# Residual loaded by the stages that use it, the last attention's weights loaded one stage earlier, and the output bias added inside the tile loop

## The chip, the cores and the metric

The kernel runs on 1 core of one Trainium2 chip. Its time is the device time of one execution in microseconds (us); several executions are taken and their median is compared.
## The reference, cut to what matters

The residual `x` is [2, 1024, 256] in float32, the context `ctx` [2, 77, 256]. Eight blocks follow, each added to the residual:

```
x = x + attn0(ln(x), ctx)          # 16 heads of 16, boolean mask: (softmax(q k^T / 4 + mask) v) Wo + bo
x = x + fp8_linear(ln(x))
x = x + attn1(ln(x), ctx)          # 16 heads of 64, keys and queries normalised
x = x + top2_experts(ln(x))        # 8 experts, the best 2 of each token
x = x + transformer(ln(x), ctx)    # self attention, cross attention, feed-forward, each with layer norm
x = x + choice_experts(ln(x))      # 8 experts, each takes its 1024 best tokens
x = x + attn3(ln(x), ctx)          # as attn0, float mask times -1e15
x = x + int8_feed_forward(ln(x))
```

The feed-forward at the end is written out to HBM as the result.

## The kernel before

**Stages.** The 2048 rows are 16 tiles of 128 (`NT`), a tile's row in `k.x` is 256 wide, and a group (`G`) is 4 tiles. `program` runs its stages one after the other, each a block of its own with one instruction stream per engine, written by hand; an engine runs its stream in order and waits on semaphores. Between two stages all engines meet: SP's stream must be over too, and then the stage's semaphores are cleared on POOL and all engines meet again (`Semaphores.clear`, L724 and L725). The whole residual stays in SBUF as `k.x`.

**The residual.** `load_residual` is a stage of its own: one DMA of 2 MB for `k.x` (L3407), seven constants (L3410), and a wait for all of them. The two stages with experts add their results by indirect DMAs into a table in HBM (`t2_total`, `ch_total`); when the last addition has landed, SP loads 2 MB back into `k.x` (L1149, L2414) and waits, and only then is the stage over. The next stages are `transformer_block` and the second `narrow_attention`. The transformer block starts on DVE with the layer norm's moments of four tiles (`first_moments`, L1976), and reads the other tiles four at a time later.

**The narrow attention** (`narrow_attention`, tags `L0_` and `L3_`) has a prologue and a tile loop. SP issues the weights first. In the prologue PE's stream is: keys and values (L3127, wait for `kv_loaded`); `turn_rows(0)` (L3118, transposes of the first group's normalised rows `h`); then for each group g: `queries(g)` (L3138), `turn_rows(g + 1)`, and `value_blocks` (L3155 and L3157), which needs `vbd` from POOL. DVE's stream is `normalise` of tiles 0 to 7 (statistics L3018 and L3021, then a chain of 12 small instructions in which each waits for the one before, L3025 and L742 to L751, then `h` at L3332), the masked keys `kbd` (L3339), and `normalise` of tiles 8 to 15. POOL clears `vbd` (L3303), copies `head_of` (L3304), builds `vbd` in four instructions (L3311) when the values are there, then adds the output bias `bo` to `x` in four instructions of a group each (L3319), each behind that group's `h`, and then enters the tile loop with one subtraction of the row maximum per tile (L3322). In the loop DVE takes the scores and finds the maxima three tiles ahead (L3357, L3365), divides and adds the result into `x` (L3380, which also waits for `bo_added`), and in the first attention it prepares the wide attention's weights beside it (`centre`, L95 to L107). In the first attention POOL's first `vbd` instruction has a change of its library in front (MODIFY_POOL_CONFIG, at 15.3 us).

Of the kernel before, what the change touches and what calls it, by code (L numbers as in the profile page):

```python
# [12 lines left out]
U8 = mybir.dt.uint8  # L13
# [661 lines left out]
class Attention:  # L675

    def __init__(self, tag, wq, wk, wv, wo, bo, bq, bk, bv, mask, mask_is_bool, beside=None):
# [3 lines left out]
        self.scale = 16 ** -0.5  # L682
# [399 lines left out]
def top2_experts(nc, k, i):  # L1082
    with ExitStack() as ctx:
# [5 lines left out]
        total = nc.dram_tensor("t2_total", (ROWS, D), F32, kind="Internal").ap()  # L1089

# [32 lines left out]
        restored = sem("restored")  # L1123
# [9 lines left out]
        def _(sp):  # L1133
# [15 lines left out]
            sp.dma_start(k.x[:], total[0:T, :].rearrange("(t p) d -> p t d", p=P)).then_inc(restored, 16)  # L1149
            sp.wait_ge(restored, 16)  # L1150
# [421 lines left out]
def transformer_block(nc, k, i):  # L1572
    scale = float(D) ** -0.5
    with ExitStack() as ctx:
# [32 lines left out]
        dve_chain, pool_chain = sem("dve_chain"), sem("pool_chain")  # L1607
        block = ctx.enter_context(nc.Block())
# [45 lines left out]
        def _(sp):  # L1654
            sp.dma_start(after[:], i["after128"]).then_inc(after_loaded, 16)
# [312 lines left out]
        def _(dve):  # L1968
# [21 lines left out]
            def first_moments(n):  # L1990
                rows = [k.x[:, unit(a)[0] * BT + unit(a)[1] + u, :] for a in (2 * n - 2, 2 * n - 1) for u in range(DUO)]
                if n >= 3:
# [353 lines left out]
def choice_experts(nc, k, i):  # L2346
    with ExitStack() as ctx:
# [5 lines left out]
        total = nc.dram_tensor("ch_total", (T, D), F32, kind="Internal").ap()  # L2353
        ps = ctx.enter_context(nc.psum_tensor("ch_ps", [P, 8, BANK], F32))
# [45 lines left out]
        restored = sem("restored")  # L2400
# [630 lines left out]
def narrow_attention(nc, k, a):  # L3031
# [3 lines left out]
    with ExitStack() as ctx:  # L3035
# [6 lines left out]
        wq, wk, wv = sb("wq_sb", [P, KC, D]), sb("wk", [P, KC, D]), sb("wv", [P, KC, D])  # L3042
        wo, bo, bq = sb("wo", [P, HC16, D]), sb("bo_sb", [P, D]), sb("bq_sb", [P, HC16])
        cols = sb("cols", [P, 2, HC16])
# [11 lines left out]
        n_masks = B if a.mask_is_bool else NT  # L3056
        neg = sb("neg", [P, n_masks, KEYS])
        if a.mask_is_bool:
            mask_u8 = sb("mask_u8", [P, B, KEYS], U8)
# [449 lines left out]
```

## Time and profile before

| | |
|---|---|
| median of 3 runs | 1848.33 us (1845.6 to 1849.25) |
| the profiled execution: its own time | 1844.21 us |
| its span in the trace | 1842.4 us |
| mean granted clock of TensorE | 0.87 |
| PE busy | 1444.0 us (78% of the span) |
| DVE busy | 1128.4 us (61%) |
| ACT busy | 747.4 us (41%) |
| POOL busy | 649.3 us (35%) |
| last attention, first DVE instruction to next stage's first | 1570.65 to 1730.01 us |
| transformer block, likewise | 870.40 to 1157.61 us |

The busy times are sums over stages with different limits; a change at a stage's edge is read from the timeline at that edge. The profiled execution took 1.8 us more than its span, and 4.1 us less than the median.

### The profile page before, as it was taken

To read this page: it belongs to the slowest core of one execution; us is meant where nothing else is said; L and a number is where in the kernel's file an instruction comes from. 1 tells how busy PE (TensorE), PEld (TensorE's weight loads), DVE (VectorE), ACT (ScalarE), POOL (GpSimd) and SP (SyncE) were. 2 spreads that over 40 slices of the span, in tenths; PEclk is the share of its full clock that TensorE was granted. 3 is DMA by queue.
4 is the path that set the end of the run, shared out by engine and by line. 5 is a ranking of instruction groups with operands and counts; after the bars stand their busy time and mean duration, and the time that the engine had idled before them with its cause. 6 is when DMAs were issued, how large, how long until landed. Compare 5 with 4: busy or idle time off the path is not lost. (4 is left out here: it accounts for less than half of the span.)

```text
span 1842.4 us, 24857 instructions
## 1 busy us (share of the span) xinstructions
PE 1444.0 (78%) x9292; PEld 1238.7 (67%) x9295; DVE 1128.4 (61%) x2410; ACT 747.4 (41%) x1292; POOL 649.3 (35%) x404
## 2 busy tenths in 40 slices
PE   5897288999655999995798986427999996789454
PEld 3686177888555999995577765416888886578322
DVE  6385865886544777763546453575666652556568
ACT  2343354444104777672445332103343431244356
POOL 3242214556301555552113222012655554433000
PEclk8799589999857999997699998558999998779778
DMA  5000000000116777763200000302545434200101
GB/s 173 1 2 5 0 2 0 1 1 1 60 46 207 227 223 216 219 204 67 70 1 1 1 1 0 128 21 83 99 96 109 98 61 69 60 1 1 48 0 46
DMA packets 93966, 121.99 MB, mean 66 GB/s; under 512 B 12092, under 2 KB 79063, under 8 KB 93847
## 3 DMA queue, kind: packets, MB, share of 16 engines
q1 hardware_dynamic: 72727, 91.56, 15.6%
q0 software_dynamic: 21120, 28.85, 8.7%
q8 instruction: 75, 1.23, 0.3%
q14 instruction: 44, 0.36, 0.1%
HBM read 94.95 MB, written 25.43 MB: 65 GB/s over the span
## 5 line engine op out<-in xcount | busy, mean ns | idle before, releaser
L1168 POOL DMA_INDIRECT t_total<-t_y,t_index x46 | 99.7, 2167 | 137.8 <-DVE t_y L1289 127.9
L2437 POOL DMA_INDIRECT ch_total<-ch_y,ch_index x64 | 103.8, 1622 | 124.2 <-DVE ch_y L2616 109.3
L3322 POOL TENSOR_TENSOR L_s<-L_s,L_mx 128x1232 f32<-128x1232 f32 x32 | 77.3, 2416 | 147.6 <-DVE L_mx L3365 147.6
L732 PE MATMUL t_ps<-t_hT_hi,t_w_hi 128*128 128x256 f32 x368 | 106.6, 290 | 7.4 <-DVE t_w_lo L1277 6.0
L732 PE MATMUL ch_ps<-ch_hT_hi,ch_w_hi 128*128 128x512 f32 x256 | 103.8, 405 | 8.8 <-DVE ch_hid L2642 5.4
L2556 ACT ACTIVATE ch_silu<-ch_ps 128x512 f32<-128x512 f32 x64 | 38.3, 599 | 177.5 <-PE ch_ps L734 177.5
L732 PE MATMUL t_ps<-t_w_hi,t_act_hi 128*128 128x256 f32 x368 | 105.8, 287 | 0.0
L733 PE MATMUL t_ps<-t_hT_lo,t_w_hi 128*128 128x256 f32 x368 | 105.3, 286 | 0.0
L734 PE MATMUL t_ps<-t_hT_hi,t_w_lo 128*128 128x256 f32 x368 | 105.3, 286 | 0.0
L734 PE MATMUL t_ps<-t_w_hi,t_act_lo 128*128 128x256 f32 x368 | 104.2, 283 | 0.0
L733 PE MATMUL t_ps<-t_w_lo,t_act_hi 128*128 128x256 f32 x368 | 104.1, 283 | 0.0
L734 PE MATMUL ch_ps<-ch_hT_hi,ch_w_lo 128*128 128x512 f32 x256 | 102.1, 399 | 0.0
L733 PE MATMUL ch_ps<-ch_hT_lo,ch_w_hi 128*128 128x512 f32 x256 | 102.1, 399 | 0.0
L2642 DVE TENSOR_TENSOR ch_hid<-ch_silu,ch_ps 128x512 f32<-128x512 f32 x64 | 43.6, 686 | 86.0 <-ACT ch_silu L2556 68.8
L3357 DVE TENSOR_TENSOR L_s<-L_ps,L_neg 128x616 f32<-128x616 f32 x64 | 48.2, 794 | 77.3 <-PE L_ps L3168 77.0
L3188 PEld LDWEIGHTS L_ps<-L_vb,L_pT 128*128 128x128 f32 (+1 forms) x640 | 79.9, 205 | 16.2 <-ACT L_pT L3290 16.2
L3188 PE MATMUL L_ps<-L_vb,L_pT 128*128 128x51 f32 (+2 forms) x640 | 83.6, 290 | 8.0 <-ACT L_pT L3290 8.0
L533 POOL TENSOR_TENSOR L_s<-L_s,L_kb 128x1232 f32<-128x1232 f32 x16 | 45.3, 2831 | 105.2 <-DVE L_s L595 105.2
L2427 POOL DMA_INDIRECT ch_hg<-ch_rows,ch_index x64 | 69.9, 1092 | 33.4 <-issue 18.9
L323 PE MATMUL L_ps<-L_vw,L_pT 128*128 128x256 f32 (+1 forms) x320 | 73.9, 387 | 7.4 <-DVE x L611 5.0
L1301 DVE TENSOR_TENSOR t_act_lo<-t_whole,t_act_hi 128x512 fp32r<-128x512 f32 x92 | 61.6, 689 | 26.2 <-ACT t_whole L1263 23.4
L1158 POOL DMA_INDIRECT t_hg<-t_rows,t_index x46 | 49.9, 1084 | 78.2 <-issue 76.7
(517 smaller groups left out, 4475.0 us busy)
## 6 DMA issues: line engine op xcount, KB each, us to landing
t_w_in<-in_L_ffn_w1T SPq DMA_DIRECT2D x23, 1024.0 KB, 4.9
t_w_in<-in_L_ffn_w2T SPq DMA_DIRECT2D x23, 1024.0 KB, 5.7
ch_w_in<-in_L_ffn_w SPq DMA_DIRECT2D x24, 512.0 KB
x<-in_x SPq DMA_DIRECT2D x1, 2048.0 KB, 8.1
t_total<-x SPq DMA_DIRECT2D x1, 2048.0 KB
t_rows<-t2d_h SPq DMA_DIRECT2D x1, 2048.0 KB
x<-t_total SPq DMA_DIRECT2D x1, 2048.0 KB, 8.0
tb_w<-in_L_xattn_w SPq DMA_DIRECT2D x2, 1024.0 KB, 11.2
```

What stands on the lines that cost most here:

```text
L323: ins = nc.tensor.matmul(ps[:, 7, 0:D], pT[0:rows, n % 2, f, :], vw[0:rows, b, f, :], start=(f == 0), stop=(f == FC - 1))
L732: nc.tensor.matmul(out, sh, mh, start=start, stop=False)
L733: nc.tensor.matmul(out, sh, ml, start=False, stop=False)
L734: return nc.tensor.matmul(out, sl, mh, start=False, stop=stop)
L1158: nc.gpsimd.indirect_dma_start(out=hg[:, j % 3, u, :], out_offset=None, in_=rows, in_offset=bass.IndirectOffsetOnAxis(ap=index[:, 2 * j + ...
L1168: nc.gpsimd.indirect_dma_start(out=total, out_offset=bass.IndirectOffsetOnAxis(ap=index[:, 2 * j + u:2 * j + u + 1], axis=0), in_=y[:, j % ...
L1301: nc.vector.tensor_tensor(act_lo[:, j % 2, 2 * q:2 * q + 2, :], whole[:, q % 2], act_hi[:, j % 2, 2 * q:2 * q + 2, :].bitcast(F32), ALU.su ...
L2427: nc.gpsimd.indirect_dma_start(out=hg[:, s % 3, u, :], out_offset=None, in_=rows, in_offset=at(s, u)).then_inc(gathered[s % 3], 16)
L2437: nc.gpsimd.indirect_dma_start(out=total, out_offset=at(s, u), in_=y[:, s % 2, u, :], in_offset=None, compute_op=ALU.add).then_inc(added[s ...
L3188: ins = nc.tensor.matmul(ps_o()[:, h0 * HEAD:h1 * HEAD], pT[0:rows, n % 2, f, :], vb[0:rows, b, f, 0:(h1 - h0) * HEAD], start=(f == 0), st ...
L3322: nc.gpsimd.tensor_tensor(s[:, n % G], s[:, n % G], spread(mx[:, n % G, :], 2, [P, H, KEYS]), ALU.subtract).then_inc(shifted, 1)
L3357: nc.vector.tensor_tensor(s[:, n % G, c * 8:(c + 1) * 8, :].rearrange("p (j i) n -> p j i n", i=2), ps[:, 0:BANDS, c * 2 * KEYS:(c + 1) * ...
```

## The change

`load_residual` goes. The first narrow attention issues on SP: tiles 0 to 3 of `x` (512 KB), four constants (`ident`, `ctxT`, `head_mask16`, `head_select`; three others, that no stage read, are not loaded any more), the key and value weights, tiles 4 to 15 in three pieces, and then the other weights. `top2_experts` and `choice_experts` don't load `k.x` back. `transformer_block` loads it in eight pieces of 256 KB ahead of its constants (only `after` stands behind the first two), and `first_moments` waits for the two pieces of its four tiles. The second narrow attention loads it in four pieces of 512 KB; its weights and its mask get their place in SBUF (`allocate`, with semaphores of their own, as in the first) before `choice_experts`, whose SP stream issues them (10 DMAs) behind the last expert's weights. In both narrow attentions `normalise` is cut into tiles 0 to 3 and, behind `kbd` and a wait for all other pieces, tiles 4 to 15; and the bias is added group by group in the tile loop, each addition in front of the subtraction of the group's first tile.

```diff
+    def allocate(self, nc, ctx):
...
+    def load_keys(self, sp):
...
+    def load_rest(self, sp):
...
@@ top2_experts, sync
             for n in range(2):
                 sp.wait_ge(added[n], 32 * len(range(n, TILES, 2)))
-            sp.dma_start(k.x[:], total[0:T, :].rearrange("(t p) d -> p t d", p=P)).then_inc(restored, 16)
-            sp.wait_ge(restored, 16)
@@ transformer_block, sync
-            sp.dma_start(after[:], i["after128"]).then_inc(after_loaded, 16)
+            for n in range(UNITS // 2):
+                for b in range(B):
+                    ts = slice(b * BT + n * DUO, b * BT + (n + 1) * DUO)
+                    sp.dma_start(k.x[:, ts, :], k.top2_total.rearrange("(t p) d -> p t d", p=P)[:, ts, :]
+                                 ).then_inc(x_loaded[n], 16)
+                if n == 0:
+                    sp.dma_start(after[:], i["after128"]).then_inc(after_loaded, 16)
@@ choice_experts, sync
             for e in range(1, E):
                 load_weights(sp, e)
+            following.load_keys(sp)
+            following.load_rest(sp)
             for n in range(2):
                 sp.wait_ge(added[n], 16 * G * (GROUPS // 2))
-            sp.dma_start(k.x[:], total.rearrange("(t p) d -> p t d", p=P)).then_inc(restored, 16)
-            sp.wait_ge(restored, 16)
+            following.loads_done(sp)
@@ narrow_attention, sync
+            rows(0)
+            if not early:
+                a.load_keys(sp)
+            for g in range(1, NG):
+                rows(g)
+            if not early:
+                a.load_rest(sp)
@@ narrow_attention, gpsimd
-            for g in range(NG):
+            def add_bias(g):
                 pool.wait_ge(h_ready, (g + 1) * G)
                 xg = k.x[:, g * G:(g + 1) * G, :]
                 nc.gpsimd.tensor_tensor(xg, xg, spread(bo[:], 1, [P, G, D]), ALU.add).then_inc(bo_added, 1)
             for n in range(NT):
+                if n % G == 0:
+                    add_bias(n // G)
@@ narrow_attention, vector
-            normalise(range(0, NT // 2))
+            dve.wait_ge(x_loaded[0], 16)
+            normalise(range(0, G))
+            a.wait_constants(dve)
             dve.wait_ge(kv_ready, HC16)
...
-            normalise(range(NT // 2, NT))
+            for g in range(1, NG):
+                dve.wait_ge(x_loaded[g], 16)
+            normalise(range(G, NT))
@@ program
-        load_residual(nc, k, i["x"], [
...
+            lambda: last.allocate(nc, late),
+            lambda: choice_experts(nc, k, i, last),
+            lambda: narrow_attention(nc, k, last, k.choice_total),
+            lambda: late.close(),
             lambda: int8_feed_forward(nc, k, i, out),
```

**DVE's stream in the prologue of the last attention, before** (statistics of a tile, their sum-up, the first three of the 12 chained instructions, `h`, `kbd`, and the second half without its chain):

```order
L3018 BN_STATS L_st<-x 128x6 x8
L3021 BN_AGGR L_mv<-L_st 128x2 x8
L3025 TENSOR_SCALAR L_var<-L_mv 128x8
L742 TENSOR_SCALAR L_tmp<-L_var 128x8
L744 TENSOR_SCALAR L_rstd<-L_tmp 128x8
L3332 TENSOR_SCALAR L_h<-x,L_mv,L_rstd 128x256 x8
L3339 SCALAR_TENSOR_TENSOR L_kbd<-L_kt,head_mask 128x616 x4
L3018 BN_STATS L_st<-x 128x6 x8
L3332 TENSOR_SCALAR L_h<-x,L_mv,L_rstd 128x256 x8
L3348 TENSOR_SCALAR L_neg<-L_neg 128x1232
```

**and now:**

```order
L3065 BN_STATS L_st<-x 128x6 x4
L3068 BN_AGGR L_mv<-L_st 128x2 x4
L3072 TENSOR_SCALAR L_var<-L_mv 128x4
L782 TENSOR_SCALAR L_tmp<-L_var 128x4
L784 TENSOR_SCALAR L_rstd<-L_tmp 128x4
L3384 TENSOR_SCALAR L_h<-x,L_mv,L_rstd 128x256 x4
L3393 SCALAR_TENSOR_TENSOR L_kbd<-L_kt,head_mask 128x616 x4
L3065 BN_STATS L_st<-x 128x6 x12
L3384 TENSOR_SCALAR L_h<-x,L_mv,L_rstd 128x256 x12
L3404 TENSOR_SCALAR L_neg<-L_neg 128x1232
```

The first part shrinks from eight tiles to four and the second grows from eight to twelve: tiles 4 to 7 have moved from ahead of `kbd` to behind it. The first attention has the same two streams.

**POOL's stream in the last attention, before** (`vbd` is the masked value matrix, `bo_sb` the bias, `L_s` the scores):

```order
L3303 MEMSET L_vbd 128x2880
L3304 COPY L_head_of<-ident 16x1232
L3311 TENSOR_TENSOR L_vbd<-L_vt,head_mask 128x616 x4
L3319 TENSOR_TENSOR x<-x,L_bo_sb 128x1024 x4
L3322 TENSOR_TENSOR L_s<-L_s,L_mx 128x1232 x16
```

**and now:**

```order
L3350 MEMSET L_vbd 128x2880
L3352 COPY L_head_of<-ident 16x1232
L3359 TENSOR_TENSOR L_vbd<-L_vt,head_mask 128x616 x4
L3368 TENSOR_TENSOR x<-x,L_bo_sb 128x1024
L3374 TENSOR_TENSOR L_s<-L_s,L_mx 128x1232 x4
```

Three of the four additions have moved from ahead of the 16 subtractions to between them, one ahead of each four; the first stays where it was. Then come the next addition and the next four subtractions, and so on.

## Rows read from the trace of the kernel before

**Rows 1.** The page, part 1: busy us (share of span) and instructions.
```profile
PE 1444.0 (78%) x9292; PEld 1238.7 (67%) x9295; DVE 1128.4 (61%) x2410; ACT 747.4 (41%) x1292; POOL 649.3 (35%) x404
```

**Rows 2.** Waits of SP's queue, whole span: us in total, times, longest.
```profile
SPq L2347 <- DMA x<-ch_total: 7.9, 1, 7.9
```

**Rows 3.** Timeline of the start: start us, us, engine, line, op [idle <-releaser].
```profile
1.25 2.10 SPq L3410 DMA_DIRECT2D ident<-in_ident  x1
...
13.09 0.43 SPq L3094 DMA_DIRECT2D L_cols<-in_L_xattn_bv  x1
...
14.09 1.20 POOL L3304 COPY L_head_of<-ident 16x1232 f32<-16x1232 f32 x1
...
15.98 2.42 PE L3127 MATMUL L_ps<-ctxT,L_wk 128*128 128x154 f32 x8 [15.98 <-DMA L_cols<-in_L_xattn_bv]
...
25.96 4.75 POOL L3311 TENSOR_TENSOR L_vbd<-L_vt,head_mask 128x616 f32<-128x616 f32 x4 [10.66 <-issue]
...
27.24 1.15 DVE L742 TENSOR_SCALAR L_tmp<-L_var 128x8 int32<-128x8 int32 x1
...
30.68 2.33 POOL L3319 TENSOR_TENSOR x<-x,L_bo_sb 128x1024 f32<-128x1024 f32 x1
...
30.77 2.27 DVE L749 SCALAR_TENSOR_TENSOR L_tmp<-L_tmp,L_var 128x8 f32<-128x8 f32 x1
...
30.81 0.77 PE L3155 MATMUL L_ps<-ident,L_vbd 128*128 128x128 f32 x2 [3.77 <-issue]
```

**Rows 4.** The page's DMA issues: line, engine, op xcount, KB each, median us to landing.
```profile
t_w_in<-in_L_ffn_w1T SPq DMA_DIRECT2D x23, 1024.0 KB, 4.9
...
x<-ch_total SPq DMA_DIRECT2D x1, 2048.0 KB, 8.3
```

**Rows 5.** Timeline where the transformer block starts.
```profile
861.23 0.38 SPq L1149 DMA_DIRECT2D x<-t_total  x1
...
870.40 1.41 DVE L1976 BATCH_NORM_STATS2 tb_st<-x 128x6 f32<-128x256 f32 x4 [15.61 <-PEq L725]
```

**Rows 6.** Timeline where the last attention starts.
```profile
1561.11 0.37 SPq L2414 DMA_DIRECT2D x<-ch_total  x1
...
1570.65 2.71 DVE L3018 BATCH_NORM_STATS2 L_st<-x 128x6 f32<-128x256 f32 x8 [18.17 <-PEq L725]
...
1575.40 2.42 PE L3127 MATMUL L_ps<-ctxT,L_wk 128*128 128x154 f32 x8 [23.64 <-DMA L_cols<-in_L_xattn_bv]
...
1576.54 2.67 DVE L3332 TENSOR_SCALAR L_h<-x,L_mv,L_rstd 128x256 f32<-128x256 f32 x8
...
1579.12 2.92 DVE L3339 SCALAR_TENSOR_TENSOR L_kbd<-L_kt,head_mask 128x616 f32<-128x616 f32 x4
...
1579.91 0.67 ACT L3266 ACTIVATE L_vt<-L_ps,L_cols 128x154 f32<-128x154 f32 x2 [1.32 <-PE L_ps L3127]
1580.73 5.94 POOL L3311 TENSOR_TENSOR L_vbd<-L_vt,head_mask 128x616 f32<-128x616 f32 x4 [6.47 <-ACT L_vt L3266]
...
1586.77 0.46 PE L3155 MATMUL L_ps<-ident,L_vbd 128*128 128x128 f32 x2
```

**Rows 7.** Windows: stretch, us, busy (x) of PE, PEld, DVE, ACT, POOL, PEclk, DMA share, GB/s.
```profile
30.80:62.70 31.90, 31.46 (x124) 21.00 (x124) 10.36 (x17) 9.75 (x28) 9.32 (x4) 0.84 0.02 3
1586.80:1618.10 31.30, 30.82 (x132) 19.93 (x136) 11.23 (x19) 11.27 (x30) 9.78 (x4) 0.88 0.00 1
1618.10:1638.50 20.40, 15.81 (x122) 12.84 (x117) 12.84 (x15) 6.79 (x9) 9.00 (x4) 0.51 0.00 1
```

**Rows 8.** Timelines of DVE behind the first attention and behind the wide one.
```profile
176.97 1.41 DVE L859 BATCH_NORM_STATS2 f_st<-x 128x6 f32<-128x256 f32 x4 [1.14 <-PEq L725]
...
492.13 1.08 DVE L1433 BATCH_NORM_STATS2 t2d_st<-x 128x6 f32<-128x256 f32 x3 [1.57 <-PEq L725]
```

**Rows 9.** Timeline of POOL in the first attention's tile loop.
```profile
136.30 3.16 POOL L3322 TENSOR_TENSOR L_s<-L_s,L_mx 128x1232 f32<-128x1232 f32 x1 [2.64 <-DVE L_mx L3365]
```

**Rows 10.** Waits inside the expert choice, its last 120 us.
```profile
DVE ch_hg L2593 <- DMA ch_hg<-ch_rows,ch_index: 7.8, 4, 4.5
```

More of the change, by code:

```diff
@@ L675, with __init__ @@
 class Attention:
-    def __init__(self, tag, wq, wk, wv, wo, bo, bq, bk, bv, mask, mask_is_bool, beside=None):
+    def __init__(self, tag, wq, wk, wv, wo, bo, bq, bk, bv, mask, mask_is_bool, beside=None, constants=()):
         self.tag, self.wq, self.wk, self.wv, self.wo, self.bo = tag, wq, wk, wv, wo, bo
@@ new lines, in load_keys @@
+    def load_keys(self, sp):
+        for dst, src in self.constants:
+            sp.dma_start(dst, src).then_inc(self.constants_loaded, 16)
+        sp.dma_start(self.wk_sb[:], self.wk.rearrange("(c p) e -> p c e", p=P)).then_inc(self.kv_loaded, 16)
+        sp.dma_start(self.wv_sb[:], self.wv.rearrange("(c p) e -> p c e", p=P)).then_inc(self.kv_loaded, 16)
+        sp.dma_start(self.cols[:, 0, :], self.bk).then_inc(self.kv_loaded, 16)
+        sp.dma_start(self.cols[:, 1, :], self.bv).then_inc(self.kv_loaded, 16)
@@ L685, with loads_done, wait_constants @@
+    def loads_done(self, sp):
+        sp.wait_ge(self.kv_loaded, 64)
+        sp.wait_ge(self.q_loaded, 32)
+        sp.wait_ge(self.o_loaded, 48)
+    def wait_constants(self, engine):
+        if self.constants:
+            engine.wait_ge(self.constants_loaded, 16 * len(self.constants))
 class Chain:
@@ L1607, in transformer_block @@
         dve_chain, pool_chain = sem("dve_chain"), sem("pool_chain")
+        x_loaded = [sem(f"x_loaded{n}") for n in range(UNITS // 2)]
         block = ctx.enter_context(nc.Block())
@@ L3055, in narrow_attention @@
         rden, o, oT = sb("rden", [P, 2, H]), sb("o", [P, 2, H, hd]), sb("oT", [P, 2, HC16, P])
[L3056 to L3059, printed above, removed]
         ps = ctx.enter_context(nc.psum_tensor(a.tag + "ps", [P, 8, BANK], F32))
-        kv_loaded, q_loaded, o_loaded = sem("kv_loaded"), sem("q_loaded"), sem("o_loaded")
+        kv_loaded, q_loaded, o_loaded = a.kv_loaded, a.q_loaded, a.o_loaded
+        x_loaded = [sem(f"x_loaded{g}") for g in range(NG)]
         kv_psum, kv_ready, cleared, kbd_ready, vbd_ready = (sem("kv_psum"), sem("kv_ready"), sem("cleared"),
@@ L3105, in _ @@
                 a.beside.loads_done(sp)
-            sp.wait_ge(kv_loaded, 64)
-            sp.wait_ge(q_loaded, 32)
-            sp.wait_ge(o_loaded, 48)
+            a.wait_constants(sp)
+            a.loads_done(sp)
+            for g in range(NG):
+                sp.wait_ge(x_loaded[g], 16)
         @block.tensor
@@ L3396, in _ @@
             dve.wait_ge(out_added, NT)
-def load_residual(nc, k, x, consts):
-    with ExitStack() as ctx:
-        loaded = Semaphores(nc, ctx, "residual_")("loaded")
-        block = ctx.enter_context(nc.Block())
-        @block.sync
-        def _(sp):
-            sp.dma_start(k.x[:], x.rearrange("(t p) d -> p t d", p=P)).then_inc(loaded, 16)
-            n = 1
-            for dst, src in consts:
-                sp.dma_start(dst, src).then_inc(loaded, 16)
-                n += 1
-            sp.wait_ge(loaded, 16 * n)
 def program(nc, i, out):
@@ L3437, in program @@
                 tag="L0_", wq=i["L0_Wq"], wk=i["L0_Wk"], wv=i["L0_Wv"], wo=i["L0_Wo"], bq=i["L0_xattn_bq"], bk=i["L0_xattn_bk"],
-                bv=i["L0_xattn_bv"], bo=i["L0_xattn_bo"], mask=i["mask_BxS2_bf0"], mask_is_bool=True, beside=wide)),
+                bv=i["L0_xattn_bv"], bo=i["L0_xattn_bo"], mask=i["mask_BxS2_bf0"], mask_is_bool=True, beside=wide,
+                constants=constants), i["x"]),
             lambda: fp8_product(nc, k, i),
```

73 lines of the change are left out of this document (41 added, 32 removed).

## The prediction

> **What bounds the kernel now.** I first read the busy shares [rows 1]: PE is busy for 78% of the span, no engine for all of it, so no single engine sets the time and the edges of stages count in full. Next come the waits of SP's queue [rows 2]: at the edge before the last attention SP waits 7.9 us for the 2 MB of `x`, and all engines wait with it, since a stage ends with its SP stream. Then I read the timeline at three edges. At the start, PE's first matmul waits until 15.98 for a transfer issued at 13.09 [rows 3], behind a whole stage that only loads. At the transformer block, 9.17 us pass between the issue of `x` at 861.23 and DVE's first instruction on it [rows 5]. At the last attention the same takes 9.54 us, and PE's keys wait 4.75 us more for weights [rows 6]. Last I read what follows inside: from the first value block to the first scores PE is busy for 31.46 of 31.90 us in the first attention and 30.82 of 31.30 in the last [rows 7]. So in both attentions the question is **when the first value block starts** and at which clock PE works from there; what starts earlier ahead of it is worth only what reaches it.
>
> **Transfers.** 1 MB lands 4.9 us after its issue, 2 MB 8.3 us after [rows 4]: 3.4 us per MB. So 512 KB land in about 3.2 us, if pieces land in the order of their issue.
>
> **Transformer block (C).** Its engines can start 1.2 us after the last table addition has landed: at the last attention the 2 MB took 0.37 of issue and 7.9 of wait, and DVE started 1.2 after that [rows 2, 6]. That is 862.4 here. Two pieces, issued 0.45 apart, land by 866.0; DVE starts 4.4 us earlier than at 870.40. The other six pieces delay the constants by 6 issues (2.8 us) and 1.5 MB, but the block starts 8 us earlier and its start is a chain through DVE, ACT and PE, which keeps the gain. **−4.4 us** (bounds −4.9 and −3.5).
>
> **Start (A).** SP issues `x`, then `ident`, which holds the queue from 1.25 to 3.35 [rows 3], then seven transfers at 0.47 each, the last of them `bv`, at about 6.25. The keys start 2.89 behind it, as before: 9.15 instead of 15.98, 6.8 earlier. But the first value block comes later in PE's stream than `turn_rows(1)`, and that needs tiles 4 to 7, now behind `kbd`. DVE: `kbd` from 13.6 (6.8 earlier) to 16.6; statistics of 12 tiles at 0.34 (2.71 for 8 [rows 6]), 4.1, and their sum-up 1.0, to 21.7; then the chain of 12 small instructions at 0.2. POOL gets in the way. An instruction of 0.17 us took 1.15 beside a `vbd` instruction of 1.19 (4.75 for 4), and 2.27 beside a bias addition of 2.33 [rows 3]: each small DVE instruction waits for the POOL instruction that is running. `vbd` starts 10.6 behind the change of library, that is behind the copy (15.29, now 7.9): 18.5. It holds POOL to 23.25, and the first bias addition to 25.6. So the chain's first three instructions end at 22.1, 23.3 and 25.6, nine more take 1.8, four `h` 1.33 (2.67 for 8 [rows 6]), and PE can start value blocks at 28.95 instead of 30.81: −1.9. The idle time before `vbd` can be read otherwise: 4.8 behind the values (21.1, by the distance of 5.2 from keys to values [rows 6]). Then it is 19.2, and the sum gives −1.2. I take **−1.5 us**; the ends are 0 (`vbd` as late as 21 or later, the library change taking 13 us in place of 10.6) and −5.2 (`vbd` done before the chain begins).
>
> The Trainium skill, GPSIMD Engine Reference, in its passage on wrapper-ucode dispatch, says that the first call to a freshly loaded library kernel pays about 6 us. By that price instead of 4.8, `vbd` would start at 20.3 and this term would be −0.2, an estimate from the page.
>
> **Last attention (D).** The block opens at 1562.4, 8.3 earlier; the weights are there. Keys start at once, values are ready 5.2 later, at 1567.6 (1579.91 + 0.67 against 1575.40 [rows 6]), and `vbd` runs 1567.7 to 1572.45. DVE has its four tiles at 1565.6: statistics 1.35, sum-up 0.4, one chained instruction. The next four each end behind a `vbd` instruction, the last at 1572.5: 4.0 us lost, which before the same chain did not lose, since `vbd` came after it. Seven more take 1.4, `h` 1.33, `kbd` 2.92: 1578.1. I let `kbd` pass the first bias addition, because before `kbd` took 2.92 unbroken while POOL's `vbd` took 5.94 instead of 4.75 [rows 6]. Then 12 tiles of statistics (4.1), sum-up (1.0), chain (2.4) and four `h` (1.33): 1587.0, transposes to 1587.2. Before the value block started at 1586.77. **+0.4 us**: the 8.3 us are eaten by 4.0 of port conflict and by four tiles moved behind `kbd`. Bounds: −3.6 without the conflict, +2.7 if the addition gets between two `kbd` instructions.
>
> The Trainium skill, SBUF — State Buffer, on the two sides of SBUF, says that whichever of the two engines starts first holds the port pair "for the whole instruction"; that speaks of one instruction, not of a run of four. By it the addition (2.33) could come after the first `kbd` instruction, and D would be +2.7; the unbroken 2.92 [rows 6] speaks against it.
>
> **Clock on that stretch (E).** PE will idle ahead of value block 0 for some 3.7 us (queries end near 1583.3 at the lower clock, `turn_rows(1)` gets its rows from 1586.0). The first attention has such a gap (3.77 [rows 3]), and behind it a mean clock of 0.84 over 31.9 us against 0.88 here [rows 7]; the lower level for 10.2 us instead of 7.5, each costing half: **+1.4 us**. Ends: 0, and +6.5, if the lower level lasts 20.4 us as it does right behind this stretch [rows 7].
>
> **Meetings of all engines (B).** Behind the first attention one meeting and clear costs 1.14 us, behind the wide one, where there are two, 1.57 [rows 8]: 0.43 for one more. The change adds two (two sets of semaphores in the first attention, `late.close()` behind the last); the one that goes lies in A. **+0.9 us**, or up to +1.5 as some clears take two instructions.
>
> **At nothing.** The bias additions inside the loop: POOL has 2.64 idle before a subtraction in the tight part of the first attention [rows 9], an addition takes 2.33, and DVE's loop reads PSUM; without that cover each costs at most its 2.33. The ten loads in the expert choice: 1.9 MB beside gathers for which DVE waits 7.8 us in 120 [rows 10]; at most +1.5.
>
> **Sum:** −1.5 + 0.9 − 4.4 + 0.4 + 1.4 = −3.2 us, from 1844.2 of the profiled execution to 1841.0. That execution stands 4.1 under the median of 1848.3, so the forecast for a median is **1845.1 us**. About 0.2% (3.7 us) is what a measurement of this kernel can tell from no change, so this lies just inside it.
>
> **Rivals.**
> - *The early opening pays in the last attention too*: DVE's chain runs clear of `vbd` (D −3.6), no gap (E 0). −1.5 + 0.9 − 4.4 − 3.6 = −8.6: 1839.7. For it: the whole 8.3 us are there. Against: values are ready just as the chain starts. Chance 0.17.
> - *The bias addition breaks into `kbd`*: +2.3, sum −0.9, 1847.4. For it: 5.94 in all shows that POOL was let in somewhere. Against: `kbd`'s 2.92 unbroken [rows 6]. Chance 0.12. The page on SBUF words it this way.
> - *The lower clock lasts through the last prologue*: E +6.5, sum +1.9, 1850.2; it decides from E = 4.6 on. For it the 20.4 us next door, against it the first attention [rows 7]. Chance 0.12.
> - *The change doesn't do what it says: pieces land together*, not in order. SP issues them back to back, so the first could land only with the last, after 8.3 us. C goes to 0, D rises by 5.1, A by about 0.8: sum +7.1, **slower**, 1855.4. It outweighs the rest once a first piece lands over 1.5 us later than 3.2 in both blocks. Against: the times [rows 4] grow with the size, as in a stream. Chance 0.08.
> - *`vbd` comes so late in the first attention that PE waits as long as now*: A 0, sum −1.7, 1846.6. For it: more transfers run beside the library change than before. Chance 0.06. The GPSIMD page's price points this way, with −0.2 for A.
>
> The forecast's own case has 0.45 and reaches from −6 to −0.5. Faster by over 0.2%: the first rival and half of the forecast's case, 0.40. Slower: the unordered pieces and a third of the clock's case, 0.12. Within: 0.48. The range, 1839.5 to 1852.0, takes in the first rival, the clock's and the bounds of C and B; it leaves out the unordered pieces and the far tails.
>
> **What would show it.** In the changed kernel: first keys near 9, DVE's first statistics of the transformer block 3.2 to 3.7 behind the first `x` piece's issue; in the last attention four small DVE instructions of about 1.1 us, and the first value block 24 to 25 us behind the block's opening against 16.1 before; a gap of PE ahead of it. Wrong, if that distance is under 21, if `kbd` takes over 4 us, or if stages without an edit differ by more than 2 us, which only PE's clock would explain.

## The result, and the profile after

| | before | after |
|---|---|---|
| median of 20 runs each | 1846.1 us (1834.6 to 1853.6) | 1852.1 us (1844.3 to 1857.9) |
| ratio after to before, 95% interval | | 1.0035 (1.0018 to 1.0052) |
| profiled execution: span, mean granted clock | 1842.4 us, 0.870 | 1850.7 us, 0.865 |

By the ratio the change made the kernel about 6.5 us slower, by the two medians 6.0 us. The prediction was 3.2 us faster, 1845.1 from a median of 1848.3, with a range that ends at 1852.0; the median of 1852.1 lies just outside. The two profiled executions stand 8.3 us apart. One of e7's 12 executions took 3684 us, and its ratio below leaves it out.

Waits of SP's queue in the changed kernel, of the whole span (us in total, times, longest), at the ends of the expert stage (L1123) and of the expert choice (L2393):

```profile
SPq L1123 <- DMA t_total<-t_y,t_index: 6.3, 1, 6.3
SPq L1123 <- PEq L1123: 3.8, 1, 3.8
SPq L2393 <- PEq L2393: 1.7, 1, 1.7
```

The load of `x` is gone from both ends, as meant [rows 2]. But a wait of 3.8 us and one of 1.7 stand in its place, in which SP has nothing left to do and the other engines are not there yet. The view of one line, L1123 in the changed kernel, shows who is late (engine, operation; ns min/median/max, first and last start in us). Each engine's stream in a stage ends with a DRAIN, and behind it the engine goes to the meeting:

```profile
L1123 PEldq DRAIN  x1: 2345/2345/2345, 852.9 to 852.9; - x1
L1123 DVEq DRAIN  x1: 725/725/725, 855.3 to 855.3; - x1
L1123 POOLq DRAIN  x1: 9192/9192/9192, 857.1 to 857.1; - x1
L1123 SPq COMPARE_BRANCH  x1: 41/41/41, 862.5 to 862.5; - x1
```

The name PEq in the wait is only the nearest event; PE had been done since 855.2. **It is POOL's DRAIN**: 9.19 us from 857.1, so until 866.3, while SP was through at 862.5. The same view of the kernel before, at its line L1083, and of the end of its expert choice, L2347:

```profile
L1083 POOLq DRAIN  x1: 9190/9190/9190, 855.8 to 855.8; - x1
L1083 SPq COMPARE_BRANCH  x1: 41/41/41, 869.3 to 869.3; - x1
```

```profile
L2347 POOLq DRAIN  x1: 10357/10357/10357, 1552.5 to 1552.5; - x1
L2347 SPq COMPARE_BRANCH  x1: 33/33/33, 1569.4 to 1569.4; - x1
```

So both drains were there before, just as long, and ended at 865.0 and 1562.9, inside SP's waits for `x`. The change took away the cover and not the drain.

Timeline of the changed kernel where the transformer block starts. The opening of a stage is its first instruction or issue behind the meeting, here 867.34:

```profile
858.72 1.56 POOL L1206 DMA_INDIRECT t_total<-t_y,t_index  x1 [0.31 <-issue]
867.34 0.89 SPq L1697 DMA_DIRECT2D x<-t_total  x2
...
870.87 1.40 DVE L2021 BATCH_NORM_STATS2 tb_st<-x 128x6 f32<-128x256 f32 x4 [14.89 <-DMA x<-t_total]
```

From the end of POOL's last scatter (860.28) to DVE's first statistics 10.59 us pass; before it was 11.37 (859.03 to 870.40, [rows 5]).

Timeline of the changed kernel at its start:

```profile
0.75 0.45 SPq L3139 DMA_DIRECT2D x<-in_x  x1
...
4.71 1.40 DVE L3065 BATCH_NORM_STATS2 L_st<-x 128x6 f32<-128x256 f32 x4 [4.71 <-DMA x<-in_x]
...
7.79 2.39 PE L3174 MATMUL L_ps<-ctxT,L_wk 128*128 128x154 f32 x8 [7.79 <-DMA L_cols<-in_L_xattn_bv]
...
15.12 5.21 PE L3185 MATMUL L_ps<-L_hT,L_wq_sb 128*128 128x512 f32 x8 [2.38 <-ACT L_hT L3293]
...
20.34 4.75 POOL L3359 TENSOR_TENSOR L_vbd<-L_vt,head_mask 128x616 f32<-128x616 f32 x4 [13.29 <-issue]
20.38 1.21 DVE L782 TENSOR_SCALAR L_tmp<-L_var 128x12 int32<-128x12 int32 x1
...
25.16 2.26 DVE L791 SCALAR_TENSOR_TENSOR L_rstd<-L_tmp,L_rstd 128x12 f32<-128x12 f32 x1
...
28.68 3.96 DVE L3384 TENSOR_SCALAR L_h<-x,L_mv,L_rstd 128x256 f32<-128x256 f32 x12
...
29.24 1.94 PE L3164 MATMUL L_ps<-ident,L_h 128*128 128x128 f32 x8 [8.90 <-DVE L_h L3384]
30.97 0.64 PE L3202 MATMUL L_ps<-ident,L_vbd 128*128 128x128 f32 x2
```

The keys come 8.2 us earlier than before [rows 3], the first value block 0.16 us later. Ahead of the turning of rows 4 to 7, which goes before that value block, PE stands still for 8.90 us.

Timeline of the changed kernel where the last attention starts:

```profile
1564.90 2.02 SPq L3139 DMA_DIRECT2D x<-ch_total  x4
...
1568.65 1.41 DVE L3065 BATCH_NORM_STATS2 L_st<-x 128x6 f32<-128x256 f32 x4 [15.32 <-DMA x<-ch_total]
...
1570.83 1.14 DVE L782 TENSOR_SCALAR L_tmp<-L_var 128x4 int32<-128x4 int32 x1
...
1577.23 2.92 DVE L3393 SCALAR_TENSOR_TENSOR L_kbd<-L_kt,head_mask 128x616 f32<-128x616 f32 x4
1577.46 4.90 POOL L3368 TENSOR_TENSOR x<-x,L_bo_sb 128x1024 f32<-128x1024 f32 x1 [3.16 <-DVE L_h L3384]
...
1579.53 6.36 PE L3185 MATMUL L_ps<-L_hT,L_wq_sb 128*128 128x512 f32 x8 [1.16 <-ACT L_hT L3293]
...
1588.08 1.77 PE L3164 MATMUL L_ps<-ident,L_h 128*128 128x128 f32 x8 [2.19 <-DVE L_h L3384]
1589.65 0.64 PE L3202 MATMUL L_ps<-ident,L_vbd 128*128 128x128 f32 x2
```

The first value block is 24.75 us behind the opening at 1564.90. From POOL's last scatter to it 29.91 us pass; before it was 27.87.

Windows from the first value block to POOL's first subtraction, in the first and in the last attention (us, busy of PE, PEld, DVE, ACT, POOL, granted clock, DMA share, GB/s), of the kernel before, then of the changed one:

```profile
30.81:66.74 35.93, 33.68 (x156) 22.62 (x156) 13.30 (x21) 9.75 (x28) 9.31 (x5) 0.83 0.01 3
1586.77:1622.23 35.46, 33.21 (x156) 21.55 (x156) 14.23 (x23) 11.89 (x30) 9.81 (x5) 0.84 0.00 0
```

```profile
30.97:69.07 38.10, 35.85 (x157) 23.43 (x156) 4.78 (x11) 10.69 (x29) 0.00 (x0) 0.77 0.00 0
1589.65:1627.32 37.67, 35.41 (x157) 23.41 (x156) 5.51 (x11) 11.98 (x30) 0.01 (x1) 0.77 0.00 1
```

The same 156 weight loads take 2.2 us more in each, at a clock of 0.77 instead of 0.83 and 0.84.

In the table each run's one profiled execution is cut at first instructions of stages; "scatter" is the end of POOL's last scatter in a stage. The first eight rows and the remainder give the 8.3 us.

| stretch, us | before | after | difference |
|---|---|---|---|
| start to first value block | 30.81 | 30.97 | +0.2 |
| on to the first subtraction | 35.93 | 38.10 | +2.2 |
| on to the fp8 product | 110.19 | 110.46 | +0.3 |
| fp8 product and wide attention | 315.15 | 313.76 | -1.4 |
| last scatter of the expert stage to DVE | 11.37 | 10.59 | -0.8 |
| last scatter of the choice to value block | 27.87 | 29.91 | +2.0 |
| on to the first subtraction | 35.46 | 37.67 | +2.2 |
| int8 stage and output | 112.47 | 115.15 | +2.7 |
| all the rest | 1163.18 | 1164.13 | +0.9 |

The fourth and the eighth row hold no edit. Their differences have opposite signs and are of the size by which executions of one kernel differ: the int8 stage and output took about 115 us in e1, which leaves them and the last attention as before, and about 113 in e2, which keeps the whole change. So the 2.7 us can't be laid to the change. Single profiles are good for edges, and medians for sums.

### The profile page after: what moved, and what is told of

Its sections match the earlier page's. It is cut to its first block and busy times, and to the rows that moved or that the text cites. A ratio compares the mean times of both kernels' runs of the same rounds, so it can differ in the third digit from the quotient of the medians.

```text
span 1850.7 us, 24893 instructions
## 1 busy us (share of the span) xinstructions
PE 1453.3 (79%) x9292; PEld 1241.0 (67%) x9295; DVE 1121.4 (61%) x2410; ACT 746.6 (40%) x1292; POOL 649.3 (35%) x404
## 5 line engine op out<-in xcount | busy, mean ns | idle before, releaser
L3235 PEld LDWEIGHTS L_ps<-L_vb,L_pT 128*128 128x128 f32 (+1 forms) x640 | 75.9, 196 | 16.5 <-ACT L_pT L3337 16.5
L3235 PE MATMUL L_ps<-L_vb,L_pT 128*128 128x51 f32 (+2 forms) x640 | 79.5, 282 | 8.6 <-ACT L_pT L3337 8.5
L772 PEld LDWEIGHTS t_ps<-t_hT_hi,t_w_hi 128*128 128x128 f32 x368 | 71.8, 195 | 8.2 <-issue 6.1
```

The costliest lines, as they stand in the source:

```text
L772: nc.tensor.matmul(out, sh, mh, start=start, stop=False)
L3235: ins = nc.tensor.matmul(ps_o()[:, h0 * HEAD:h1 * HEAD], pT[0:rows, n % 2, f, :], vb[0:rows, b, f, 0:(h1 - h0) * HEAD], start=(f == 0), st ...
```

## Experiments

Each ratio is to runs of the kernel before on the same chip; in microseconds, 0.001 is 1.8. By these intervals a difference between two of the kernels is known to about 5 or 6 us, and to 7 where e5 is one of them.

| kernel | ratio | 95% interval |
|---|---|---|
| as changed | 1.0035 | 1.0018 to 1.0052 |
| e1: before, transformer block's part alone | 0.9991 | 0.9969 to 1.0013 |
| e2: changed, its `x` issued ahead | 1.0030 | 1.0009 to 1.0051 |
| e3: the same at both edges | 1.0003 | 0.9982 to 1.0024 |
| e4: changed, split 8 and 8 | 0.9955 | 0.9936 to 0.9975 |
| e5: e3 and e4 together | 0.9918 | 0.9887 to 0.9950 |
| e6: changed, PE's pauses filled | 0.9997 | 0.9973 to 1.0020 |
| e7: changed, bias ahead of the loop | 1.0047 | 1.0022 to 1.0072 |
| e8: changed, weights loaded late | 1.0051 | 1.0024 to 1.0077 |
| e9: as e6, fewer matmuls | 1.0013 | 0.9987 to 1.0040 |
| e10: e5, with matmuls in two pauses | 0.9926 | 0.9902 to 0.9950 |
| e11: changed, library change early | 1.0015 | 0.9992 to 1.0037 |
| e12: changed, 8 and 8 in the first attention | 0.9979 | 0.9961 to 0.9997 |

**e1, the transformer block's part alone**, on the kernel before:

```diff
-            sp.dma_start(k.x[:], total[0:T, :].rearrange(...)).then_inc(restored, 16)
-            sp.wait_ge(restored, 16)
...
+            for n in range(UNITS // 2):
+                for b in range(B):
+                    sp.dma_start(k.x[:, ts, :], k.top2_total...).then_inc(x_loaded[n], 16)
```

> The kernel before with one part of the change alone: the expert stage ends without loading x, the transformer block loads it in eight pieces. Theory 'drain': GpSimd's drain at the end of the expert stage (9.19 us in both traces) ends 3.8 us behind the landing of the last table addition; before it lay under the 8.1 us load of x, now all engines wait for it, so DVE's first statistics stand 8.4 us behind SP's last wait (9.2 before) and the whole kernel is 0.8 us faster, not to be told from no change. The recorded prediction's step: 4.8 us behind it, the kernel 4.4 us faster (ratio 0.9976). Rival 'pieces slow': the opening of the block is 1.2 us behind the landing, and it is the first piece that lands late, over 6 us behind its issue.

DVE's first statistics stand 10.38 us behind the last scatter (before 11.37), so this part is worth 1.0 us at its edge, not 4.4, as 'drain' said. By the ratio the kernel is 1.7 us faster, which can't be told from no change.

**e2 and e3, the same loads under the drain's cover.** The pieces are issued by SP at the end of the stage ahead, on semaphores that are held outside it:

```diff
             for n in range(2):
                 sp.wait_ge(added[n], 32 * len(range(n, TILES, 2)))
+            for n in range(4):
+                for b in range(B):
+                    sp.dma_start(k.x[:, ts, :], total...[:, ts, :]).then_inc(k.tb_loaded[n], 16)
...
```

> The changed kernel, with the eight pieces of the transformer block issued at the end of the expert stage's SP stream, on semaphores that outlive the stage. Theory 'drain': the pieces land while GpSimd drains; the block opens 4.9 us behind the last landing as in the changed kernel, the first statistics follow at once, 4.9 to 5.0 behind it instead of 8.4, and the kernel is 3.4 us faster than the changed one. Rival 'code': the meeting is late because engines fetch the next stage's instructions, for which it does not matter where the pieces are issued, but the transfers then slow that fetch: the opening moves later by 1 us or more and the gain is under 2.5 us.

> As the run before, and the four pieces of the last attention issued at the end of the expert choice's SP stream as well. Theory 'drain': the attention opens 2.9 us behind the last landing, its first piece is there 3.7 us behind it, so DVE starts 2.9 us earlier than in the changed kernel; its small instructions are then mostly done before GpSimd's vbd instructions begin, which saves 2.5 us more, and the first value block stands 22.3 us behind the last landing instead of 27.6: 5.3 us faster than the run before, if PE's clock behind it is the same. Rival 'clock': PE has the same pauses ahead of the first value block and repays them at the lower clock: under 3 us faster although the first value block is earlier.

Timeline of e2 at the edge:

```profile
863.26 1.56 POOL L1211 DMA_INDIRECT t_total<-t_y,t_index  x1 [0.30 <-issue]
867.03 3.96 SPq L1192 DMA_DIRECT2D x<-t_total  x8
...
872.34 0.35 SPq L1700 DMA_DIRECT2D tb_after<-in_after  x1
...
872.38 1.41 DVE L2021 BATCH_NORM_STATS2 tb_st<-x 128x6 f32<-128x256 f32 x4 [11.94 <-PEq L765]
```

DVE now starts as the block opens, 7.56 us behind the last scatter instead of 10.59: 3.0 of the 3.4 us expected. e3 shows the same (7.65). The opening is 7.5 us behind the scatter, 7.1 in the changed kernel: POOL's DRAIN ends at 870.8, and SP is still issuing the eight pieces until 870.99, so the drain's cover is just used up. By the ratios e2 is only 0.9 us faster than the changed kernel, less than the intervals resolve. At the last attention e3 starts DVE 6.33 us behind the last scatter instead of 8.91, but the first value block 28.65 instead of 29.91: 1.3 us, not 5.3. DVE's chain was not clear of POOL: four small instructions took 1.06 to 1.22 us each, one beside POOL's copy and three beside `vbd`, and the first four `h` took 2.25 together for 1.38. By the ratios e3 is 5.9 us faster than the changed kernel, beyond the 5 us that the intervals leave, and 5.0 faster than e2, which they just don't resolve. That this is the 5.3 expected is luck: only 1.3 of it came by the way expected; the stretch on to the first subtraction took 34.8 us in e3's profile and 37.9 in e2's, at a granted clock of 0.86 and 0.77.

**e4, the split**, and **e12, the split in the first attention alone:**

```diff
-            dve.wait_ge(x_loaded[0], 16)
-            normalise(range(0, G))
+            for g in range(NG // 2):
+                dve.wait_ge(x_loaded[g], 16)
+            normalise(range(0, NT // 2))
...
-            normalise(range(G, NT))
+            normalise(range(NT // 2, NT))
```

> The changed kernel with 8 and 8 tiles normalised before and behind kbd, as before, instead of 4 and 12, in both attentions. Theory 'order': in the last attention DVE has h of tiles 4 to 7 near 14 us behind the opening instead of 23, and the first value block is 21 to 23 us behind the opening instead of 24.8; in the first attention vbd becomes the last condition and the first value block stands at 25.2 to 27 instead of 31.0. Together 5 to 9 us faster than the changed kernel. Rival 'clock': what PE gains at the start it repays at the lower clock, under 3 us in all.

> The changed kernel with the even split of 8 and 8 tiles in the first attention alone. Theory 'order and clock': the first attention is as in the kernel with both splits even (first value block at 26.5, 33.7 us to the first subtraction, 106 to 110 behind it), so 8 to 12 us of the 14.9 are won here: ratio to the kernel before 0.997 to 0.999; the last attention is as in the changed kernel (29.9 us from the last scatter to the first value block, near 37.7 behind it). Rival: the two attentions share the gain by halves, 7 to 8 us here, ratio 0.9993 to 1.0, and the rest of the first profile's difference is PE's clock, which differs from one execution to the next.

e4 is faster than the changed kernel by 0.0080, 14.8 us, more than the 5 to 9 expected, and 8.3 us faster than the kernel before. **With the even split the same change is a gain.** e12 gets 10.3 us of the 14.8, inside the 8 to 12 expected, but its interval also takes in the rival's 0.9993. Its profile has the first value block at 25.70 and the stretch behind it in 33.22 us, as expected; the tile loop behind took 112.5 us at a granted clock of 0.86, where 106 to 110 were expected. Timeline of e4 (its profiled execution is the fastest of its 12) at its start, and its windows over the same two stretches as above:

```profile
16.37 1.97 PE L3164 MATMUL L_ps<-ident,L_h 128*128 128x128 f32 x8 [4.30 <-DVE L_h L3384]
19.49 6.33 PE L3185 MATMUL L_ps<-L_hT,L_wq_sb 128*128 128x512 f32 x8 [1.16 <-ACT L_hT L3293]
25.66 1.04 PE L3164 MATMUL L_ps<-ident,L_h 128*128 128x128 f32 x8
26.54 0.39 PE L3202 MATMUL L_ps<-ident,L_vbd 128*128 128x128 f32 x2
```

```profile
26.54:60.29 33.75, 31.50 (x158) 20.71 (x156) 9.11 (x23) 10.66 (x30) 1.80 (x1) 0.88 0.01 3
1572.87:1606.62 33.75, 31.51 (x158) 20.72 (x156) 8.66 (x30) 11.94 (x31) 0.00 (x0) 0.88 0.00 0
```

The first queries begin 4.4 us later than in the changed kernel, and yet the first value block comes 4.4 us earlier, because tiles 4 to 7 are no longer behind `kbd` and 12 tiles of statistics. In the last attention it stands 28.08 us behind the last scatter, for 29.91. PE goes from the queries to the value blocks without a pause, and behind them it is granted 0.88 instead of 0.77, another 4 us in each attention.

**e6 and e9, the pauses filled.** PE gets matmuls that nobody reads (nothing of the result changes); e9 has fewer of them. `early` is true in the last attention, whose weights are loaded early:

```diff
+            def idle_work(times):
+                pe.wait_ge(kv_ready, 2 * HC16)
+                for _ in range(times):
+                    nc.tensor.matmul(ps[:, 7, 0:KC * D], k.ident[:], wk[:]..., start=True, stop=True)
...
+            idle_work(12 if early else 0)
             turn_rows(0)
...
+                if g == 0:
+                    idle_work(4 if early else 16)
```

> The changed kernel, with PE given matmuls whose result nobody reads where it now pauses ahead of the first value block: 16 of 128x512 behind the first queries of the first attention, 12 behind the values and 4 behind the first queries of the last. Theory 'clock': the lower clock behind the pause (17.1 of the 38.1 us up to the first subtraction in the first attention, 17.2 of 37.7 in the last) goes away for the most part, the first value block itself stays within 1 us of where it is, and the stretch behind it takes 33.5 to 35 us as with the even split: 5 to 9 us faster than the changed kernel in all. Rival 'order': what the even split won is work of DVE that comes earlier; then the filled kernel is as slow as the changed one, or slower.

> As the filled kernel, with the unread matmuls cut to what fits the pauses (one call of 128x512 took 0.87 us there, so 16 of them took 13.9 us and moved the first value block 3.2 us back): 9 behind the first queries of the first attention, 6 behind the values and 2 behind the first queries of the last. Theory 'clock': the first value blocks stand where the changed kernel has them (31.0, and 29.9 behind the last scatter), and the stretches behind them are as short as in the filled kernel (33.8 and 33.2): 8 to 10 us faster than the changed kernel, 2 to 4 faster than the kernel before. Rival: with pauses of a few us left, the lower clock comes back, and it is as the changed kernel.

Windows of e6 over the two stretches:

```profile
34.18:67.93 33.75, 31.50 (x158) 20.69 (x156) 2.96 (x4) 10.64 (x29) 0.00 (x0) 0.88 0.00 1
1592.73:1625.89 33.16, 30.90 (x158) 20.25 (x156) 5.26 (x10) 11.93 (x30) 0.00 (x1) 0.90 0.00 1
```

PE does more work and its first value block is 3.2 us late in the first attention (within 1 us was expected), but the kernel is 0.0038, 7 us, faster than the changed one. The stretches behind are as short as with the even split. So PE's idle time ahead sets the clock behind. How much depends on more than the length of the last pause. Windows over the stretch in e2's first attention, whose streams are those of the changed kernel, and in e8's last:

```profile
30.44:66.44 36.00, 33.76 (x157) 22.54 (x156) 4.79 (x11) 10.69 (x29) 0.00 (x0) 0.83 0.00 0
1587.44:1623.32 35.88, 33.63 (x157) 22.48 (x156) 5.33 (x11) 11.97 (x30) 0.00 (x0) 0.83 0.00 0
```

The pauses right ahead of these were 6.44 and 6.13 us; behind the changed kernel's 8.90 and 2.19 the stretches took 38.10 and 37.67 at 0.77. e9 takes 32.06 us in the first attention; in the last, where 3.70 us of pause were left, 36.13 at a clock of 0.83. By the ratios it is 4 us faster than the changed kernel, half of what was expected and not resolved by the intervals. In its profile the last attention's tile loop took 4.4 us more (112.7 instead of 108.3), at a granted clock of 0.86 instead of 0.89; the edit leaves that loop as it was.

**e7 and e8, the parts costed at nothing.**

```diff
-                if n % G == 0:
-                    add_bias(n // G)
+            for g in range(NG):
+                add_bias(g)
```

```diff
-            following.load_keys(sp)
-            following.load_rest(sp)
...
-            following.loads_done(sp)
...
-            lambda: last.allocate(nc, late),
```

> The changed kernel with GpSimd's four bias additions ahead of the tile loop again, in both attentions. As recorded, the additions inside the loop cost nothing: no difference over 1.5 us in total, and the same period of 5.8 us from one subtraction to the next. Rival: each addition in the loop delays a subtraction by up to 2.3 us, three per attention; then this kernel is up to 14 us faster, and the gaps in the loop's subtractions are shorter at every fourth tile.

> The changed kernel with the last attention's weights loaded in the attention itself, the first piece of x ahead of them. Theory: kbd waits for DVE's chain, not for the keys, so the early loads win little: keys start 4 to 5 us later, vbd with them, which takes vbd out of the way of DVE's chain (3.0 us lost there now): first value block at 1.5 us either side of the changed kernel's 24.8 behind the opening, total within 1.5 us. The stage of the expert choice is within 0.5 us of now. Rival: the early weights are what opens the stage sooner, and without them it is 4 us or more slower.

Neither can be told from the changed kernel (1.0047 and 1.0051 against 1.0035). Timeline of POOL in the changed kernel's first loop:

```profile
128.00 3.16 POOL L3374 TENSOR_TENSOR L_s<-L_s,L_mx 128x1232 f32<-128x1232 f32 x1 [4.32 <-DVE L_mx L3421]
131.12 2.37 POOL L3368 TENSOR_TENSOR x<-x,L_bo_sb 128x1024 f32<-128x1024 f32 x1
133.81 3.16 POOL L3374 TENSOR_TENSOR L_s<-L_s,L_mx 128x1232 f32<-128x1232 f32 x1 [0.32 <-DVE L_mx L3421]
```

The addition fills the idle time of 2.64 before a subtraction [rows 9] and leaves 0.32; the period stays 5.81, which e7's loop has too. In e8's profile the first value block stands 30.65 us behind the last scatter, for 29.91: the early loads won 0.7 us there.

**e5, both repairs, and e10, both with filled pauses.** e5's edits are those of e3 and e4; e10 adds `idle_work(7 if early else 4)` behind the values.

> The changed kernel with both former repairs: the pieces of x issued in the stage ahead at both edges, and 8 and 8 tiles around kbd. If the two effects add: 3.0 us less than the even split alone at the transformer block (7.6 us from GpSimd's last scatter to DVE's first statistics instead of 10.6), and at the last attention DVE starts some 7.4 us behind the last scatter instead of 11.7; of these 4.3 us up to 4 go to waits of DVE's small instructions for GpSimd's vbd instructions, which then run at the same time. So 3.5 to 7 us faster than the even split alone, 10 to 14 faster than the kernel before (ratio 0.992 to 0.995). Rival 'clock': the profiles differ at the openings as said, and the total by under 2 us, as PE works longer at the lower clock.

> The kernel with the pieces issued ahead at both edges and the even split, and 4 (first attention) and 7 (last) unread matmuls behind the values, where PE pauses for 4.8 and 7.7 us. Theory 'clock': the first queries, now 5.5 and 6.6 us at the lower clock, take 3.7; in the last attention the first value block comes 2.5 to 2.9 us earlier, in the first it is held by vbd, which ends at 27.2, and gains nothing: 1.5 to 4 us faster than without the matmuls, if the lower clock does not come back later. Rival: it does, and the total is the same within 1.5 us.

e5 is 15 us faster than the kernel before, a little more than the 10 to 14 expected. By the ratios it is 6.8 faster than e4, just at the edge of what the intervals resolve, and about as much as the same loads gave without the even split (e3 against the changed kernel, 5.9). In its profile 3.1 of this is at the transformer block (7.44 against 10.56), but in the last attention the first value block comes 28.15 behind the last scatter against 28.08: DVE starts 4.0 us earlier and loses it all to `vbd` and the queries' lower clock. e10 brings the first value blocks to 24.89 and 26.45 (from 27.24 and 28.15), as expected, and the total is not faster than e5's (0.9926 against 0.9918), which is what the rival said. In its profile the last tile loop took 113.1 us instead of 108.9, at a granted clock of 0.86 instead of 0.89. As e9, e11 and e12 have loops as long, whether the filled pause is the cause isn't shown.

**e11, the change of library early:**

```diff
+            nc.gpsimd.memset(warm[:], 0.0).then_inc(warmed, 1)
             nc.gpsimd.memset(vbd[:], 0.0).then_inc(cleared, 1)
+            pool.wait_ge(warmed, 1)
+            nc.gpsimd.tensor_tensor(warm[:, 0:1], warm[:, 0:1], warm[:, 1:2], ALU.mult).then_inc(warmed, 1)
             a.wait_constants(pool)
```

> The changed kernel with one 128x1 multiplication ahead of GpSimd's copy of ident in both attentions, so that the change of library begins near 3.3 us instead of 7.1. Theory 'port': in the first attention term A came out at 0 because the change of library took 13.2 us instead of the recorded 10.6, so that vbd and a bias addition lay across DVE's chain (4 instructions of 1.1 to 1.2 us and one of 2.3). Now vbd starts at 15 to 18 and ends at 20 to 22.5, the chain takes 2.4 to 5 us instead of 8.3, and the first value block comes at 25 to 28 instead of 31.0. The last attention stays as it is. Total 3 to 6 us faster than the changed kernel, more if PE's clock recovers as with the even split. Rival: the first value block waits for tiles 4 to 7 behind the 12-tile statistics anyway, and moves by less than 2 us.

```profile
11.73 0.18 POOL L3354 TENSOR_TENSOR L_warm<-L_warm 128x1 f32<-128x1 f32 x1 [8.46 <-issue]
11.87 1.20 POOL L3356 COPY L_head_of<-ident 16x1232 f32<-16x1232 f32 x1
13.75 6.48 POOL L3363 TENSOR_TENSOR L_vbd<-L_vt,head_mask 128x616 f32<-128x616 f32 x4 [0.67 <-ACT L_vt L3314]
```

```profile
13.15 6.00 DVE L3397 SCALAR_TENSOR_TENSOR L_kbd<-L_kt,head_mask 128x616 f32<-128x616 f32 x4 [2.76 <-ACT L_kt L3314]
...
26.52 3.96 DVE L3388 TENSOR_SCALAR L_h<-x,L_mv,L_rstd 128x256 f32<-128x256 f32 x12
```

DVE's chain now takes 2.3 us instead of 8.3, but `vbd` moved onto `kbd`, which takes 6.00 instead of 2.92. The first value block comes at 28.81, 2.2 us earlier, where 25 to 28 was expected. The kernel is 3.7 us faster by the ratios, which the intervals don't resolve. So about 2 us of the first attention's loss belonged to the late `vbd`. With the even split the first value block comes at 26.54 (e4), so the 12 tiles behind `kbd` held the first one back too.

## Why the prediction was wrong

**Transformer block (C), forecast -4.4.** The failed step is "Its engines can start 1.2 us after the last table addition has landed", taken from an edge where 7.9 us of SP's wait lay between. Without them the opening is 4.8 us behind SP's last wait, since POOL's DRAIN ends 3.8 us behind it. The pieces behaved as said (3.53 us from the first issue to the statistics, forecast 3.2 to 3.7), so "pieces land together" is out, and so is the early opening that pays in full. The part was worth 0.8 to 1.0 us at its edge; e2, e3 and e5 put it under the drain and got 2.9 to 3.1 more.

**Last attention (D), forecast +0.4.** The failed step is again the opening: 2.9 us behind SP's last wait instead of 1.2, because of the drain, which makes +2.0 of +0.4. The distance from the opening to the first value block came as worked out, 24.75 for 24 to 25, in part by luck: the first piece landed 3.75 us behind its issue for 3.2, and PE turned the rows at the lower clock, but only three chained instructions took 1.14, where four were forecast. `kbd` stayed at 2.92 and the bias addition beside it took 4.90, so that rival is out here.

**Start (A), forecast -1.5, came out +0.2.** The sum took the library's change at 10.6 us; it was 13.2, and `vbd` started at 20.34 instead of 18.5. The keys came at 7.79 instead of 9.15, since `ident` held SP's queue for 0.49 us and not for 2.10 as before, and that won nothing. This was the rival at 0.06 (`vbd` late, A = 0). The Trainium skill, GPSIMD Engine Reference, in its passage on wrapper-ucode dispatch (about 6 us for the first call to a freshly loaded kernel), gave an estimate of 20.3 and a term of -0.2, and was nearer than my rows. That it met 20.34 is luck: the values were ready at 12.8, not at 14.4 as forecast, and `vbd` started 7.5 us behind them, not 6. It is no fixed price: `vbd` began 4.8 behind the values before, and e11's change took 8.5 in all with its operands ready. 0.9 us more is PE turning rows 4 to 7 in 1.94 us, for 1.03 at the higher clock.

**Clock (E), forecast +1.4.** The mechanism, lost clock behind idle time of PE, was right; the term was too small, and it was applied to one attention only. PE's pause ahead of the first value block grew from 3.77 to 8.90 us in the first attention and from none to 2.19 in the last, and in this pair of profiles each stretch behind took 2.2 us more. e6 shows that PE's idle time is the cause: with PE busy there, 4.4 and 4.5 us of these stretches go away. In the last attention it filled the pause of 7.71 behind the values too, so it doesn't say which pause counts. The way the term was sized was not sound: it compared 0.84 with 0.88 [rows 7], but up to the first subtraction the kernel before has 0.83 and 0.84, with a pause of 3.77 and without one. The second window of rows 7 ends just where the lower clock begins.

**Meetings (B), forecast +0.9.** 1.57 us stand behind the first attention for 1.14, and 1.88 behind the last for 1.14: +1.2, inside the bounds.

**At nothing.** The bias additions and the early loads cost nothing that e7 and e8 can tell, which is to about 6 us in the total; closer than that goes only the unchanged period in the loop. The early loads won 0.7 us at their edge.

Together: C 3.6, A 1.7, D 1.6, the clock 3.0 and B 0.3 above forecast make 10.2, which takes -3.2 to 7.0; measured were 6.5. The terms come from one pair of profiles and the 6.5 from medians, so that they agree this well is in part luck. The side of the result was decided by two omissions: the drain under the removed wait, and the clock behind a pause that an earlier start makes longer. The prediction counted the four tiles moved behind `kbd` only as work that eats the early opening. e4 shows that this split decides the side by itself: without it the change wins 8.3 us, drain and all. The prediction named as a sign of being wrong that stages without an edit differ by more than 2 us; the int8 stage did, by 2.7, at a granted clock of 0.72 for 0.75 over its first 110 us. What stays open: why the lower clock lasts longer in some executions' tile loops (in the last attention 103.8 us from the first subtraction on at 0.93 in e1, 113.1 at 0.86 in e10; in the first 104.2 at 0.93 in e7, 112.5 at 0.86 in e12), which is as large as the effects studied here, and what a drain's length follows: in the changed kernel it ended 6.0 us behind the last scatter in one stage and 4.0 in the other.

## What to carry to other kernels

Before costing the removal of a wait, list every engine's last instruction at that edge, sequencer ones too, and cost the edge by the latest of them that is left: here a DRAIN behind scatters was already in the trace of before, ending 4 us ahead of SP. If a transfer can't be removed, issue it under such a drain, ahead of the meeting, rather than behind it; check that the issues themselves end with the drain. And an order that lets an engine start its first item earlier, but makes it wait longer for the next, buys a pause: count the pause and PE's clock behind it, not the start.

## What was not expected of the hardware

- POOL's DRAIN behind indirect scatters ended 5.7 to 6.1 us after the last of two (8.95 to 9.29 us long in the fourteen profiles) and 4.0 us after the last of eight (10.35 us long): in the changed kernel 3.8 and 1.7 us after SP had seen the last of them land.
- POOL and DVE on one run of instructions: in the changed kernel `kbd` ran unbroken in 2.92 us and POOL's addition took 4.90 for 2.33. In e11 `kbd` and `vbd` started within 0.6 us of each other and took 6.00 and 6.48, for 2.92 and 4.75: they took turns, with about 1.8 us for most instructions of either. The Trainium skill, SBUF — State Buffer, on the two sides of SBUF, has a lock "for the whole instruction"; e11 agrees with it. The addition ended 2.2 us behind the last `kbd` instruction, so it sat through all that were left, and the lock isn't always handed over between two of them.
- Matmuls that nobody reads made a kernel faster by 7 us, although they put the first value block 3.2 us later.
